# Fourier layers on one Trainium2 core: the inverse transform along the height cut into 64x64 quarters and placed between transposes

## The reference

```python
for sw, cw, cb in ((sw0, cw0, cb0), (sw1, cw1, cb1), (sw2, cw2, cb2), (sw3, cw3, cb3)):
    x_ft = jnp.fft.rfft2(x, norm='ortho')                        # forward transform
    out = jnp.einsum('bixy,ioxy->boxy', x_ft[:, :, :20, :20], w) # mix channels, 20x20 modes
    x1 = jnp.fft.irfft2(out_ft, s=(64, 64), norm='ortho')        # inverse transform
    x2 = jnp.einsum('bchw,oc->bohw', x, cw) + cb                 # pointwise
    x = gelu(x1 + x2)
```

## Time and profile before

| | |
|---|---|
| median of 3 runs | 6450.11 us (6440.57 to 6450.9) |
| the profiled execution's own time | 6453.83 us |
| its span, first to last instruction | 6452.0 us |
| PE busy | 5726.8 us, 89% of the span |
| DVE, ACT, POOL busy | 44%, 41%, 17% |
| mean granted TensorE clock | 0.942 of full |

### The profile page before, as it was taken

One profiled execution on the slowest core, in us unless ns is written; L12 is line 12 of the kernel. 1 busy time (PEld: TensorE's weight loads), 2 busy tenths in 40 slices (PEclk: granted clock), 3 DMA queues, 4 the chain that ended last, 5 costly groups with the idle time before them and its releaser, 6 DMA issues. The chain is left out here.

```text
span 6452.0 us, 236091 instructions
## 1 busy us (share of the span) xinstructions
PE 5726.8 (89%) x100782; PEld 4383.7 (68%) x100782; DVE 2856.1 (44%) x4430; ACT 2673.7 (41%) x5007; POOL 1098.8 (17%) x1049
## 2 busy tenths in 40 slices
PE   5999999999899899899999999999999588888888
PEld 4887788678868886887688768877886333333343
DVE  2444344344434443443344334434443565657573
ACT  2334433433353335333433343344334455555563
POOL 3220222032202221221222122203220000000000
PEclk9999999999999999999999999999999788888887
DMA  2101100111011110111010110111000100000000
GB/s 32 13 13 14 19 13 13 14 18 13 13 17 16 16 20 9 16 20 13 13 19 13 14 19 13 13 14 16 13 13 4 20 1 8 1 7 1 4 1 4
DMA packets 442836, 82.80 MB, mean 13 GB/s; under 512 B 437592, under 2 KB 437864, under 8 KB 441704
## 3 DMA queue, kind: packets, MB, share of 16 engines
q1 hardware_dynamic: 441832, 67.58, 8.4%
HBM read 63.33 MB, written 4.23 MB: 10 GB/s over the span
## 5 line engine op out<-in xcount | busy, mean ns | idle before, releaser
L217 POOL COPY x_T<-x_X 128x512 f32<-128x512 f32 x1024 | 1069.6, 1104 | 3744.7 <-ACTq L718 3573.5
L713 ACT ACTIVATE x_X<-ga 128x512 f32<-128x512 f32 x1280 | 752.1, 598 | 888.1 <-PE ga L433 679.4
L591 DVE COPY x_X<-ev 128x512 f32<-128x512 f32 x640 | 442.8, 692 | 1284.7 <-PE ev L451 1214.5
L433 PEld LDWEIGHTS ga<-pw_rhs,x_X 64*64 64x64 f32 x32768 | 605.7, 135 | 293.0 <-issue 291.1
L681 ACT ACTIVATE V<-ga 104x512 f32<-104x512 f32 x416 | 248.4, 597 | 1050.7 <-PE ga L401 1050.7
L401 PE MATMUL ev<-inv_h,D 104*104 104x128 f32 x4864 | 621.1, 277 | 36.9 <-DVE D L591 35.9
L591 DVE COPY V<-ev 104x512 f32<-104x512 f32 x608 | 420.6, 692 | 477.1 <-PE ev L401 477.1
L433 PE MATMUL ga<-pw_rhs,x_X 64*64 64x64 f32 x32768 | 601.0, 218 | 19.4 <-issue 16.9
L401 PEld LDWEIGHTS ev<-inv_h,D 104*104 104x104 f32 x4864 | 562.9, 172 | 73.6 <-DVE D L591 27.0
L463 PEld LDWEIGHTS ev<-dft_consts,x_T 128*64 128x64 f32 x16384 | 575.6, 137 | 47.7 <-issue 47.7
L463 PE MATMUL ev<-dft_consts,x_T 128*64 128x80 f32 x16384 | 594.9, 233 | 10.1 <-POOL x_T L217 9.4
(11 more groups left out here) (195 smaller groups left out, 7638.9 us busy)
## 6 DMA issues: line engine op xcount, KB each, us to landing
mix_w<-in_sw SPq DMA_DIRECT2D x128, 400.0 KB, 8.2
coords<-in_coords SPq DMA_DIRECT2D x64, 96.0 KB, 2.1
maps<-Y SPq DMA_DIRECT2D x128, 16.0 KB
raw<-maps SPq DMA_DIRECT2D x8, 256.0 KB, 3.5
out<-out_t SPq DMA_DIRECT2D x8, 256.0 KB, 3.2
w<-in_w SPq DMA_DIRECT2D x3, 512.0 KB, 6.8
fc_rhs<-in_fc_w SPq DMA_DIRECT2D x32, 0.4 KB
dft_consts<-in_dft SPq DMA_DIRECT2D x1, 336.0 KB
```

The lines of the kernel that those rows point to most:

```text
L217: pool.tensor_copy(x_T[:, :, H * bc + h0:H * bc + h0 + 16].rearrange("p c (s n) -> p c s n", n=2), blocks.rearrange("p (s a n c) -> p a c ...
L433: last = pe.matmul(ps[HALF * bp:HALF * bp + HALF, HALF * s:HALF * s + HALF], x_X[r:r + HALF, g, col:col + HALF], pw_rhs[r:r + HALF, :], st ...
L591: dve.tensor_copy(dst, src).then_inc(ev_taken, 1)
L713: x_new = act.activation(blocks.rearrange("p (s a n) -> p s a n", s=8, a=2)[:, :, bc, :], ga[n % N_GA][:, :].rearrange("p (s n) -> p s n", ...
```

## The change

It touches the 72 middle groups with g < 3 only. `inverse_h` of the next group is no longer one block of 8 banks between `forward_w` and `forward_h`. It becomes four calls of `inverse_h_pair`, each of which fills one `ev` and one `ga` bank. Where before one matmul took both images of a pair with a block diagonal matrix (104x104 weights, 128 columns), there are now four: rows 0 to 39 or 64 to 103 of D, columns of the lower or upper half, 64 columns of `inv_h`. The first three calls stand between pairs of `turn_x` banks, the fourth behind `forward_w`. `turn_d(g + 1)` moves from behind `turn_x` to behind the first pair of banks of `inverse_w_and_pointwise`. DVE and ACT empty the banks in the new order; their copies into V now take 64 points of 8 channels in place of 128 points of 4. `inverse_h` at the start of a layer and everything in the first and last phases stay as they were.

```diff
--- before.py
+++ after.py
@@ -403,6 +403,25 @@
                         last.then_inc(ga_ready if shared and i % 2 else ev_ready, 1)
                     return n["ev"], n["ga"]
 
+                def inverse_h_pair(d_at, i):
+
+                    pe.wait_ge(ev_taken, ev0 + d_at[0] + 1)
+                    pe.wait_ge(ga_taken, ga0 + d_at[1] + 1)
+                    pair = [ev_tile()]
+                    passed()
+                    pair.append(ga_tile())
+                    passed()
+                    for s in range(8):
+                        for bp, ps in enumerate(pair):
+                            r = HALF * bp
+                            for bc, m in enumerate((HALF, KR)):
+                                last = pe.matmul(ps[HALF * bc:HALF * bc + m, HALF * s:HALF * s + HALF],
+                                                 D[r:r + KR, 8 * i + s, HALF * bc:HALF * bc + m],
+                                                 inv_h[r:r + KR, r:r + HALF], start=True, stop=True)
+                            if s == 7:
+                                last.then_inc(ga_ready if bp else ev_ready, 1)
+                    return n["ev"], n["ga"]
+
                 def project_coords(g, part):
 
                     if part[0] == 0:
@@ -436,7 +455,8 @@
                                 if s == 7:
                                     last.then_inc(ga_ready, 1)
                         if i == 0 and behind is not None:
-                            behind()
+                            passed_on = behind()
+                    return None if behind is None else passed_on
 
                 def turn_x(g, part=range(TURN_X), written=None):
 
@@ -547,20 +567,26 @@
                     behind()
                     return
                 for g in range(NG):
+                    if kind != "first" and g + 1 < NG:
+                        d_at = inverse_w_and_pointwise(g, v_at, lambda: turn_d(g + 1))
+                        written = n["ga"] - NB
+                        for i in range(INV_T // 2):
+                            turn_x(g, range(2 * i, 2 * i + 2), written)
+                            if i < INV_T // 2 - 1:
+                                inverse_h_pair(d_at, i)
+                        y_at = forward_w(g)
+                        v_at = inverse_h_pair(d_at, INV_T // 2 - 1)
+                        forward_h(y_at)
+                        continue
                     if kind != "first":
                         inverse_w_and_pointwise(g, v_at)
-                    x_at = turn_x(g)
-                    more = kind != "first" and g + 1 < NG
-                    if more:
-                        d_at = turn_d(g + 1)
+                    turn_x(g)
                     ahead = kind == "first" and g + 1 < NG
                     if ahead:
                         project_coords(g + 1, range(NB // 4))
                     y_at = forward_w(g)
                     if ahead:
                         project_coords(g + 1, range(NB // 4, NB // 2))
-                    if more:
-                        v_at = inverse_h(d_at)
                     forward_h(y_at)
                 mix_next()
 
@@ -620,8 +646,12 @@
                         take(V[0:HALF + KR, :, 4 * i:4 * i + 4],
                              ev_tile()[0:HALF + KR, :].rearrange("p (c n) -> p n c", n=P))
 
-                def turn_x(g):
-                    for i in range(0, TURN_X, 2):
+                def inverse_h_pair(i):
+                    take(V[0:HALF + KR, 0:HALF, 8 * i:8 * i + 8],
+                         ev_tile()[0:HALF + KR, :].rearrange("p (c n) -> p n c", n=HALF))
+
+                def turn_x(g, part=range(0, TURN_X, 2)):
+                    for i in part:
                         if kind != "last":
                             dve.wait_ge(xt_ready, xt_done(kind, chunk, layer) + NB * g + 2 * (i // 2) + 2)
                         take(x_X[:, g, BC * i:BC * i + BC], ev_tile()[:, :])
@@ -651,14 +681,24 @@
                 else:
                     dve.wait_ge(stored, chunk * (16 * J * NG) + 16)
                 for g in range(NG):
+                    if kind == "mid" and g + 1 < NG:
+                        turn_d()
+                        for i in range(INV_T // 2):
+                            turn_x(g, [2 * i])
+                            if i < INV_T // 2 - 1:
+                                inverse_h_pair(i)
+                        forward_w()
+                        inverse_h_pair(INV_T // 2 - 1)
+                        forward_h(g)
+                        continue
                     turn_x(g)
-                    more = kind != "first" and g + 1 < NG
+                    more = kind == "last" and g + 1 < NG
                     if more:
                         turn_d()
                     if kind != "last":
                         forward_w()
                     if more:
-                        inverse_h(1 if kind == "last" else 2)
+                        inverse_h(1)
                     if kind != "last":
                         forward_h(g)
                     if kind == "last":
@@ -737,15 +777,22 @@
                                            bias=fc1_bias[:, :]).then_inc(ga_taken, 1)
                         return n + J
 
+                    def inverse_h_pair(i):
+                        act.wait_ge(ga_ready, ga0 + n + 1)
+                        act.activation(V[0:HALF + KR, HALF:P, 8 * i:8 * i + 8],
+                                       ga[n % N_GA][0:HALF + KR, :].rearrange("p (c n) -> p n c", n=HALF), ACT.Copy)\
+                            .then_inc(ga_taken, 1)
+                        return n + 1
+
                     for i in range(1, TURN_X, 2):
                         n = turn_x(i)
+                        if kind == "mid" and g + 1 < NG:
+                            n = inverse_h_pair(i // 2)
                         if kind == "last" and i == TURN_X // 2 - 1:
                             n = fc1(0)
                     if kind == "last":
                         for i in range(1, J):
                             n = fc1(i)
-                    if kind == "mid" and g + 1 < NG:
-                        n = inverse_h()
 
             phases(act, run)
 
```

## The result

The changed kernel takes 6383.73 us in the median (6376.39 to 6391.31, 4 runs) against 6447.56 (6440.57 to 6450.9, 4 runs) for the kernel before: ratio 0.9896, 95% interval 0.9885 to 0.9908. The forecast was 6317 with a range of 6248 to 6378; the time lies above it, in the band of rival 2.

A forecast was written before the change was run, and what follows sets the result against it. PE's own time was taken as the bound: 28.25 - 7.17 + 3.76 + 1.3 = 26.1 us a group, plus 0.3 for instruction feed, 26.4. Over 72 groups 133 us less gave 6317 us, range 6248 to 6378.

The forecast's parts named there:

- rival 2: In the groups, instruction feed is the new bound: gain only 0.4 to 1.1 us a group, 6370 to 6420 us; 14%.
- What bounds the kernel: In the 72 middle groups the time is PE's own: covered for 28.13 of 28.25 us, other engines far less busy.
- Quarters side by side: In `inverse_h_pair` four quarters run at once: 0.94 us a call, 3.76 a group in place of 7.17.
- rival 3: In the new calls quarters run only two at a time: 1.83 us a call, 6576 us in all; 3%.
- The switches: Between quarters, transposes and other matmul shapes in a group, each change costs 0.04 to 0.17 us; sum 1.3 a group.
- The instruction stream: From second pair to last transposes of x, fetch of PE's instructions costs 0.3 us more a group; at most 1.5.
- the slow reading: In the dense stretch, instruction packets at 4.0 us each in place of 3.6: 3.7 packets make 14.8 us, not 13.3.
- Who could be late: In the new order x_T copies keep 4 us spare, D is 5 us early, and the bank ring holds ACT's delay.
- the last Y copy: Between `forward_w` and `forward_h`, a call of about 1.1 us just covers DVE's 0.94; costed at 0 to 0.1.
- The baseline: Full groups before the change taken at 28.25 us, from which the forecast 26.4 us a group was subtracted.
- 133 forecast: Over the 72 middle groups, 1.85 us less each: 133 us saved in all.

The follow-up runs named there:

- e3_full_between: The changed kernel with all four inverse calls in the old full-width form, at the new places; 6469.69 us, ratio 1.0039 to the kernel before.
- e7_third_full: The changed kernel with the third inverse call of each full group in the old full-width form; 6317.10 us, ratio 0.9810 to the kernel before.
- e2_quarters_block: The changed kernel with all four calls of quarters in one block behind `forward_w`, the old order; 6631.58 us, ratio 1.0299 to the kernel before.
- e4_halves_block: The changed kernel with row halves (one matmul for both column quarters), all four calls in one block behind `forward_w`; 6570.33 us, ratio 1.0187 to the kernel before.

## Why the prediction was wrong

- **What bounds the kernel**: right. PE before and after; the other engines' busy times in a group are unchanged, and nothing they do is waited for more than before.
- **Quarters side by side** (0.94 us a call): right, so rival 3 is out. **The switches** (1.3 us a group): right in their sum. The rows of the changed kernel give 1.08 for a call up to transposes (forecast 1.11), 1.02 for a pair of banks (1.02), 2.33 from `turn_d` to the next shape; the stages of a group without stops, each at its median without a stop, make 25.75 us, where 26.1 less the 0.34 of stops in it is 25.76.
- **The instruction stream**: this step failed. It gave 0.3 us more than the 0.34 that the group held; the changed kernel has 27.20 - 25.75 = 1.45. The 0.8 us too few are 58 us over 72 groups, the largest part of the 67 by which the time missed the forecast. Two things were wrong in it. "At 3.6 us that is 23 us, below 26.1, so on average the feed suffices" took the shortest of the three gaps in the earlier trace rows as the rate. Their mean, 30 slices of 0.4 us for three packets, is 4.0, and the group of the changed kernel has 3.97. With it the sum is 1,680 instructions (1,608 records and some 70 register instructions) / 256 x 3.97 = 26.0 us, against 25.75 of array: no margin even on average. That is the argument of rival 2, which got 14% because weights were thought to be loaded by DMA in the mix and to slow its packets. That was a misreading of the earlier trace rows: in this window of 1004 to 1020 us nothing moved but the four instruction packets.

```profile
DMA packets 4, 0.07 MB, mean 4 GB/s; under 512 B 0, under 2 KB 0, under 8 KB 0
```

  One caution on 3.97: where PE doesn't stop, packets come as fast as PE uses them, so the spacing in a group is no clean measure of the feed. Just ahead of the stops of over 0.5 us in the changed kernel's groups (86 of them, where the feed must be the limit) the last two packets stand 3.4 to 5.0 us apart, 4.1 in the mean: the slow reading, and no constant.

  The second thing: the stops were looked for in the quarter runs; they stand wherever a block of 256 ends behind a dense stretch, `forward_h` included. The Trainium skill (Runtime: NRT & Kernel Launch, Instruction fetch mechanics) gives the block, 16 KiB or 256 instructions, and the trace agrees (7 packets, 0.11 MB); its "mostly hidden" doesn't hold here, as the shifted stops show.
- **The mix, the starts and the last groups** were costed at nothing and took 22.7 us. The 7.9 us of the starts go with the clock: a start lasts 12.8 to 13.7 us where the clock is half for 3 to 5 of them, and 15.2 us or more where it is half for 8.9 or more. The kernel before has 3 long starts in 24 layers, the changed one 7. Why there are more is open, and so are the 12.2 us of the mixes, whose length follows their half clock (60 us before, 73 after) only loosely. That their blocks stand otherwise in the stream may be part of it (e3_full_between and e7_third_full lose there too, the latter 11.3 us: 4.6, 5.6 and 1.1); it was not tested by itself.
- **Who could be late**: right. The fourth call is cover enough for the last Y copy, and D, x_T and the banks are in time.
- **The baseline**: the two groups read for the forecast (28.25, 28.19) were shorter than the mean of 72 (28.38), 9 us over the run in favour of the change. So: 133 forecast, + 9, - 58, = 84 against the 85.2 measured in the groups; - 22.7 for the rest of the layers and + 4.5 outside them make the 67.

How deep PE's reserve of instructions is stays open. It is small: the kernel before uses only 5 packets in 28.25 us, and yet it stops at the end of its pointwise stage. One shortest time per block predicts more stops for e7_third_full than came, so it seems to be more than one block. Steady use of up to about 60 instructions per us (1,585 in 26.43 us) went with 0.1 to 0.2 us of stops a group, 65 (1,680 in 25.75) with 1.45. That e7_third_full came out at the forecast number (6317) is chance: it pays 0.5 us more array time for stops that the forecast hadn't counted.

## What to carry to other kernels

Cutting a matmul into smaller ones that run side by side buys array time with instructions; count both, and take for the feed the mean spacing of the instruction packets in a stretch that stops, not the shortest. When both come out about equal, keep part of the work in the wide form and put that part into the densest stretch: here one call of four gave as much again as the whole change. Place small matmuls between slower stages; in one block the same instructions made the kernel 3% slower. Look at the granted clock of each stage before you explain a loss by waits: half clock can come without any gap in PE's work.

## What the runs showed of the hardware

- PE took about 256 instructions per 4.0 us in a stretch with stops (six packets in 23.8 us), about 64 per us; ahead of its stops the last two packets stood 3.4 to 5.0 us apart. The stops came only where a multiple of 256 instructions was reached, and moved by exactly 64 when 64 were put ahead.
- Matmuls on row halves with 104 columns of weights went by at 0.045 us a record (two records in 0.09 us), while quarters of 40 and 64 columns took 0.015. At 2.4 GHz, 104 columns are 0.043 us, so the loads of the two row halves seem to go one behind the other, and those of the column halves side by side. The Trainium skill (TensorEngine Tiling (Array Packing), Key Properties) lets tiles load and multiply in parallel; the quarters agree (0.015). The row halves agree in part: a load of 104 columns and a move of 64, all one behind the other, would be 0.070 us a record, so something overlaps, but by these numbers not load with load. That it is the loads is argued and not shown.
- An instruction of PE that only passes a semaphore already reached took 0.15 us behind the mix (9.5 us for 64).
- The granted clock fell to half within blocks of small matmuls: 0.75 over 13.6 us in e2_quarters_block, where PE also stopped, and 0.75 over a block of 7.86 us in e4_halves_block, where PE was covered throughout. It stayed at 1.00 in the groups where the same calls stood between transposes.
- At a layer's start the half clock that began in the mix lasted 3 to 5 us in most layers of the changed kernel and 9 in 7 of 24; the start took 12.8 to 13.7 us in the one case and 15.2 to 15.5 in the other.
